# Weight products of the second attention by head, the work in both passages between stages put in another order, and the router in one pass

## The reference

```python
x = x + attn(layernorm(x))            # 16 heads of 128, windowed, difference of two softmaxes
x = x + xattn(layernorm(x), ctx)      # 16 heads, low-rank keys and values from ctx
x = x + ffn(layernorm(x))             # 16 experts of 176, top 6, and a shared expert of 352

# xattn, per head h
q_big = rope((hidden @ Wq_h.T) @ w_kc_q_h)        # 256 -> 128 -> 192
q_r, k_r = q_big @ W_qr_h, rope(ctx) @ W_kr_h     # 192 -> 64, 64 -> 64
attn = softmax(q_r @ k_r.T)
out += (attn @ rope(ctx)) @ w_kc_kv_h.T @ Wo_h.T

# ffn
probs = softmax(xf @ gate_w.T)                    # 16 experts
combine = probs where among the top 6 of a token, else 0
moe = sum_e combine[:, e] * (silu(g_e) * u_e) @ w2_e.T
```

## Time and profile before

| | |
|---|---|
| Median of 3 runs | 1394.78 us (1394.64 to 1397.84) |
| The profiled execution | 1395.27 us, span 1393.4 us |
| TensorE busy | 1309.9 us, 94% of the span |
| VectorE, ScalarE, POOL busy | 847.0, 722.3, 470.7 us |
| Mean granted TensorE clock | 0.978 of full speed |
| Bytes by DMA | 64.57 MB, mean 46 GB/s |
| The chain that ended last | PE 71%, issue 12%, DVE 6%, ACT 4%, POOL 4%, DMA 2%, SPq 1% |

### The profile page before, as it was taken

The page is one execution under the profiler, slowest core; times in us unless marked ns, Lnnn a source line. Parts: engine busy times, 40 slices in busy tenths (PEclk is TensorE's granted clock), DMA queues, the critical chain, the costliest instruction groups (busy, mean ns, idle before and its releaser), DMA issues.

```text
span 1393.4 us, 27992 instructions
## 1 busy us (share of the span) xinstructions
PE 1309.9 (94%) x9948; PEld 1026.1 (74%) x9948; DVE 847.0 (61%) x1985; ACT 722.3 (52%) x2767; POOL 470.7 (34%) x466
## 2 busy tenths in 40 slices
PE   5899999999999888999999999959999999999998
PEld 3677887887887765666676666548888888888887
DVE  7788788787887576646646656755443343333433
ACT  2788887887887554444444444453333242333322
POOL 3222122212211134534534534550044253432532
PEclk9899999999999899999999999988999999999999
DMA  6011002000102101001002001010134234253130
GB/s 213 16 32 39 17 17 54 17 16 16 32 16 88 34 1 73 1 2 73 2 1 72 1 1 59 1 40 18 33 70 132 63 93 90 38 132 75 43 100 30
DMA packets 29684, 64.57 MB, mean 46 GB/s; under 512 B 6784, under 2 KB 12032, under 8 KB 28288
## 3 DMA queue, kind: packets, MB, share of 16 engines
q1 hardware_dynamic: 29568, 63.05, 16.3%
HBM read 52.42 MB, written 2.23 MB: 39 GB/s over the span
## 4 chain that ended last, share of the span: by engine, by line
PE 71%; issue 12%; DVE 6%; ACT 4%; POOL 4%; DMA 2%; SPq 1%; POOLq 0%; DVEq 0%; ACTq 0%
PE ps L515 30%; PE ps L879 9%; PE ps L698 4%; PE ps L802 4%; PE ps L631 4%; PE ps L663 3%; PE ps L792 3%; PE ps L776 3%; PE ps L784 2%; PE ps L674 2%; POOL ea L1622 2%; PE ps L654 2%; DMA cw<-comb_d 2%; ACT ea L1392 1%; PE ps L570 1%
## 5 line engine op out<-in xcount | busy, mean ns | idle before, releaser
L1751 POOL TENSOR_TENSOR sg<-sg,cw 128x512 f32<-128x512 f32 x88 | 113.6, 1291 | 278.6 <-ACT sg L1558 270.6
L1333 DVE TENSOR_TENSOR hh<-ps,sg 128x512 f32<-128x512 f32 x100 | 69.2, 692 | 182.1 <-POOL sg L1751 165.6
L1359 ACT ACTIVATE hhh<-hh 128x512 fp32r<-128x512 f32 x100 | 63.2, 632 | 209.0 <-DVE hh L1333 198.2
L1359 ACT ACTIVATE pt<-ps 128x512 f32<-128x512 f32 x128 | 76.8, 600 | 179.3 <-PE ps L784 112.9
L1392 ACT ACTIVATE ea<-ps,negmax 128x64 f32<-128x64 f32 (+1 forms) x512 | 164.6, 341 | 6.0 <-DVE negmax L1085 6.0
L515 PE MATMUL ps<-xnh,wch 128*128 128x512 f32 x400 | 159.6, 399 | 0.5 <-DVE x_sb L1046 0.5
L515 PE MATMUL ps<-xnh,wcl 128*128 128x512 f32 x400 | 159.3, 398 | 0.0
L515 PE MATMUL ps<-xnl,wch 128*128 128x512 f32 x400 | 158.5, 396 | 0.0
L1132 DVE TENSOR_TENSOR qcs<-ps,tabb 128x512 f32<-128x512 f32 x192 | 123.5, 686 | 54.6 <-PE ps L515 54.2
L1622 POOL TENSOR_TENSOR ea<-ea,rden 128x128 f32<-128x128 f32 (+1 forms) x128 | 62.2, 507 | 230.8 <-DVE rden L1041 230.8
L1629 POOL TENSOR_TENSOR eb<-eb,rsum 128x512 f32<-128x512 f32 x64 | 66.5, 1039 | 172.7 <-DVE rsum L1172 172.7
(11 more groups left out here) (149 smaller groups left out, 3436.6 us busy)
## 6 DMA issues: line engine op xcount, KB each, us to landing
raw_w<-in_rawb_dram SPq DMA_DIRECT2D x4, 2432.0 KB, 9.4
kva<-ktmp SPq DMA_DIRECT2D x64, 128.0 KB, 2.3
cw<-comb_d SPq DMA_DIRECT2D x32, 256.0 KB, 4.8
raw_w<-in_rawc_dram SPq DMA_DIRECT2D x4, 1920.0 KB, 8.1
cw<-comb_d SPq DMA_DIRECT2D x16, 224.0 KB, 4.2
raw_a<-in_wqk_dram SPq DMA_DIRECT2D x4, 768.0 KB, 4.5
cw<-comb_d SPq DMA_DIRECT2D x16, 192.0 KB, 5.9
cw<-comb_d SPq DMA_DIRECT2D x16, 160.0 KB, 5.5
```

Of the source, the lines that this page charges most:

```text
L1333: dve.tensor_tensor(hh[:, par, :], bank(C_U[par]), sg[:, par, :], ALU.mult).then_inc(c_h, 1)
L1359: return act.activation(dst, src, ACT.Copy)
L1751: pool.tensor_tensor(sg[:, par, :], sg[:, par, :], cw[:, c % 2, t, :], ALU.mult).then_inc(c_hs, 1)
```

## The change

`b_prep` makes wb by head: items 0 to 3 are the heads, two products of 192 columns each into columns 0 to 383 of a bank; ScalarE and VectorE scatter them into the row tiles in two copies and two subtractions (`b_split`, `b_columns`). Items 4 and 5 make mq for three tiles each, and VectorE alone copies it. The slots of the items in the loop stay.

The passage from A to B: chunk 4's turns go to unit 12, the six items to slots 0 and 1 of units 13 to 15, three of four context transposes to unit 15, slot 2, with banks 0, 1 and 7; the rest, qb 0 to 3 and chunk 5's turns to the second drain unit. Chunk 6's turns go to B's units 0 and 1 and chunk 7's to units 4 and 5.

The passage from B to C: chunk 9's turns go to unit 14; the first gate and up products stand in the second drain unit, the gate product between the last transposes and PV; chunks 10 and 11 are turned at k = 1 and 3. ScalarE and POOL prepare three of the five weight tiles before C and two in its first pairs. The wait for B's additions moves behind the products of k = 1.

The router takes all 16 sequences at once: the padded gate weight (32 columns) is the stationary operand, the 512 tokens of a chunk move, and the four chunks go to four column strips of one bank, at k = 4; four transposes bring the logits back to token order at k = 5; one chain of 16 steps on 256 columns; all four combine transposes at k = 8, ahead of the down product there. SP loads the next weights after the first spread instead of before the first store.

```diff
-                   ("final", 11, 0): [("ln", 4, 0)], ("final", 11, 1): [("ln", 4, 1)],
-                   ("final", 12, 0): [("prep", 0)], ("final", 12, 1): [("prep", 1)],
-                   ("final", 13, 0): [("prep", 2)], ("final", 13, 1): [("prep", 3)], ("final", 13, 2): [("prep", 4)],
-                   ("final", 14, 0): [("prep", 5)], ("final", 14, 1): [("ln", 5, 0)], ("final", 14, 2): [("ln", 5, 1)],
-                   ("final", 15, 1): [("kt2", 0)], ("final", 15, 2): [("kt2", 1)],
-                   ("drain", 0, 1): [("qb", 0), ("qb", 1), ("kt2", 2)], ("drain", 0, 2): [("kt2", 3)],
-                   ("drain", 1, 0): [("ln", 6, 0)], ("drain", 1, 1): [("qb", 2), ("qb", 3)],
-                   ("drain", 1, 2): [("ln", 6, 1)]}
+                   ("final", 12, 0): [("ln", 4, 0)], ("final", 12, 1): [("ln", 4, 1)],
+                   ("final", 13, 0): [("prep", 0)], ("final", 13, 1): [("prep", 1)],
+                   ("final", 14, 0): [("prep", 2)], ("final", 14, 1): [("prep", 3)],
+                   ("final", 15, 0): [("prep", 4)], ("final", 15, 1): [("prep", 5)],
+                   ("final", 15, 2): [("kt2", 0), ("kt2", 1), ("kt2", 2)],
+                   ("drain", 1, 0): [("kt2", 3), ("qb", 0)], ("drain", 1, 1): [("qb", 1)],
+                   ("drain", 1, 2): [("qb", 2), ("qb", 3), ("ln", 5, 0), ("ln", 5, 1)]}
...
-                   ("final", 12, 1): [("ln", 9, 0, 7), ("ln", 9, 1, 2)],
-                   ("drain", 0, 2): [("ln", 10, 0, 2), ("ln", 10, 1, 3)]}
+                   ("final", 14, 2): [("ln", 9, 0, 7), ("ln", 9, 1, 3)]}
...
             def b_prep(g_to, t, bk):
...
+                if t < HG:
+                    for kt in range(KT):
+                        last = pe.matmul(bk[:, XQ * kt:XQ * (kt + 1)],
+                                         raw_b[:, RB_WQ + t * DM + 128 * kt:RB_WQ + t * DM + 128 * (kt + 1)],
+                                         raw_b[:, RB_KCQ + t * XQ:RB_KCQ + (t + 1) * XQ], start=True, stop=True)
+                    return last
+                for k in range(XT // 2):
+                    for h, a, w, row in b_segments(XT // 2 * (t - HG) + k):
...
+                if drain and u == 1:
+                    c_up(0, 0, 0, 0)
...
+            def c_logits():
 
                 pe.wait_ge(c_gws, 16)
+                pe.wait_ge(ln_h, 3 * NC * KT)
+                for kt in range(KT):
+                    for c in range(NC):
+                        last = pe.matmul(ps[EQ * c:EQ * (c + 1), C_X[0], :], gw[:, kt, :], xnf[:, kt, CW * c:CW * (c + 1)],
+                                         start=kt == 0, stop=kt == KT - 1, skip_group_check=True)
...
+            def c_turn():
+
+                pe.wait_ge(c_gs, GATE_STEPS)
...
+                if first and k == 1:
+                    pe.wait_ge(b_y, NG * UN)
+                if first and k in (1, 3):
...
+                if first and k == 4:
+                    c_logits()
+                if first and k == 5:
+                    c_token_major()
+                if first and k == 8:
+                    c_turn()
...
-            ln_stats(2 * NC - 1)
-            dve.wait_ge(a_wo, NG * UN)
+            dve.wait_ge(a_tp, NG * UN)
             item = XT + 4
             for what in B_FIRST[item:]:
+                if what[0] == "qr":
+                    ln_low(5)
+                    ln_stats(6)
+                    dve.wait_ge(a_wo, NG * UN)
...
+                if first and k == 0:
+                    ln_norm(3 * NC - 1)
+                if first and k in (2, 4):
+                    ln_low(2 * NC + 1 + k // 2)
+                if first and k == 5:
+                    gate_take()
+                if first and 5 <= k < 8:
+                    gate(k - 5)
...
+            ln_low(2 * NC + 1)
+            c_low(0, 1)
+            c_low(0, 2)
+            ln_rstd(3 * NC - 1)
+            ln_low(2 * NC + 2)
+            ln_low(3 * NC - 1)
+            for t in range(SH_N, TG):
                 c_low(0, t)
```

More of the change, by code:

```diff
@@ L49 @@
 GATE_STEPS = 16
-GP = 2
-GB = B // GP
+EQ = 32
 RC_T = 2 * KT * 128 + DM
@@ L543, in pj_taken @@
                     pe.wait_ge(b_if, what[1] + 1)
-                else:
-                    pe.wait_ge(b_kvc, what[1] + 1)
             def b_turn(r):
                 pe.wait_ge(b_kv, 5)
+                if r < 2:
+                    pe.wait_ge(a_ex, NG * UN - 1)
+                elif r == 2:
+                    pj_taken(held.pop())
+                else:
+                    pe.wait_ge(b_kvc, 1)
                 for j in range(CB):
-                    last = pe.transpose(quads(bank(PJ))[:, j, :], kvr[:, CB * r + j, :, :], idf[:, :])
+                    last = pe.transpose(quads(bank(kt_bank(r)))[:, j, :], kvr[:, CB * r + j, :, :], idf[:, :])
                 last.then_inc(b_kvp, 1)
@@ L797, in b_unit @@
                         pe.wait_ge(b_if, b_item(g, 2, 2, ("wco", 1)) + 1)
+                    if first and u == 3:
+                        pe.wait_ge(a_y, NG * UN)
                     pe.wait_ge(b_ol, n - 2)
@@ L804, in b_unit @@
                     last.then_inc(b_wo, 1)
+                if drain and u == 1:
+                    c_up(0, 0, 0, 0)
                 slot(2)
-            def c_logits(p, bk):
-                pe.wait_ge(c_gws, 16)
-                pe.wait_ge(ln_f, (2 * NC + (p + 1) * NC // GP) * KT)
-                for i in range(GB):
-                    b = GB * p + i
-                    for kt in range(KT):
-                        last = pe.matmul(ps[:, bk, E * i:E * (i + 1)], xnf[:, kt, S * b:S * (b + 1)], gw[:, kt, :],
-                                         start=kt == 0, stop=kt == KT - 1)
-                last.then_inc(c_lg, 1)
@@ new lines, in c_token_major @@
+            def c_token_major():
+                pe.wait_ge(c_lt, 1)
+                for j in range(CB):
+                    last = pe.transpose(quads(bank(C_X[1]))[:, j, :], glt[:, S * j:S * (j + 1)], idf[:, :])
+                last.then_inc(c_lm, 1)
+            def c_turn():
+                pe.wait_ge(c_gs, GATE_STEPS)
+                for r in range(NC):
+                    last = pe.matmul(ps[0:CB * E, C_X[0], S * r:S * (r + 1)], gp[:, CB * r:CB * (r + 1), :], idf[:, :],
+                                     start=True, stop=True)
+                last.then_inc(c_ct, 1)
@@ L1173, in b_unit @@
                 slot(1)
+                if final and u == 15:
+                    ln_stats(10)
+                if drain and u == 0:
+                    ln_low(9)
+                if drain and u == 1:
+                    ln_norm(10)
                 if not (first and u < 3):
@@ L1176, in b_unit @@
                 slot(2)
+                if first and u in (2, 6):
+                    ln_low(2 * NC - 2 + u // 4)
                 if first and u == 2:
-                    ln_low(2 * NC - 1)
+                    ln_stats(2 * NC - 1)
+                if first and u == 3:
+                    ln_norm(2 * NC - 1)
                 if final and u == 7:
@@ L1235, in gate @@
                 elif i == 1:
-                    dve.wait_ge(c_ge, p + 1)
-                    step(dve.tensor_reduce(gsum[:, bs], ge[:, bs, :], axis=AX.X, op=ALU.add))
-                    step(dve.reciprocal(grec[:, bs], gsum[:, bs]))
-                    step(dve.tensor_tensor(gp[:, bs, :], ge[:, bs, :], over_e(grec[:, bs]), ALU.mult))
-                    for b in range(GB * p, GB * (p + 1)):
+                    dve.wait_ge(c_ge, 1)
+                    step(dve.tensor_reduce(gsum[:, :], ge[:, :, :], axis=AX.X, op=ALU.add))
@@ L1462, in b_take @@
                         bk = bank(2 + par)
-                    copy(wbh[:, t, :, :].rearrange("p k n -> p (k n)"), bk[:, 0:256])
-                    copy(mq[:, t, :], bk[:, 256:384]).then_inc(b_m, 1)
+                    for high, src in zip(b_split(wbh, t), b_columns(bk)):
+                        last = copy(high, src)
+                    last.then_inc(b_m, 1)
                 elif kind == "wco":
@@ L1500, in b_unit @@
                 slot(2)
-                if first and u < KT:
-                    ln_take(2 * NC - 1, u, QRB)
+                if first and u in (0, 1, 4, 5):
+                    ln_take(2 * NC - 2 + u // 4, u % 4, QRB)
             def c_high(g_to, t):
@@ L1558, in c_unit @@
                 act.activation(sg[:, par, :], bank(C_G[par]), ACT.Silu).then_inc(c_sg, 1)
-                if first and k in (7, 11):
-                    for i in range(2):
-                        c_take_comb((k - 7) // 2 + i, C_X[i])
                 act.wait_ge(c_h, v + 1)
```

287 lines of the change are left out of this document (140 added, 147 removed).

## The result

The changed kernel takes 1363.3 us (median of 4 runs, 1355.4 to 1363.8) beside 1395.7 for the kernel before: ratio 0.9749, 95% interval 0.9725 to 0.9774. In a second series on another occasion it took 1363.3 beside 1395.9, 0.9764 (0.9751 to 0.9777). So it is 32 to 33 us faster, where 42.2 were forecast. Its profiled execution took 1363.3 (span 1361.5, granted clock 0.983; before 0.978). TensorE is busy for 1279.0 us instead of 1309.9, still 94% of the span.

The account below looks back on a forecast made before the run. TensorE's work was taken to bound the loop, and its waits for other engines and lowered clock the two passages. Gains of 12.8 + 13.4 + 16.0 = 42.2 us led to 1352.6 us as a median, range 1341 to 1366.

Parts of the forecast that it names:

- rival (b): Both attentions' last units or first feed-forward tiles: ScalarE's order bites harder, 12 us less gain, 1364.6 us; chance 0.15.
- Loop, 12.8: Second attention's loop: three rebuilds of the weight products each gain 4.3 us, 12.8 us together (10 to 15).
- The stall in unit 11: Loop, unit 11: three items back to back on two banks make TensorE wait, charged 0.7 us a turn.
- First passage, 13.4: Passage from stage A to B: second attention's first scores 17.4 us earlier net, less 4 for clock: 13.4 us (8 to 18).
- The clock, charged with 4.0: First passage: clock falls after three remaining waits of 2 to 3 us would cost 4 us.
- the walk: First passage stepped through on the old clock: second attention's first scores at 513.1 instead of 531.5.
- The five waits: First passage, TensorE: 2.1, 3.2 and 2.6 us before units' products, 1.5 before the out product, 2.0 before the contraction.
- Second passage and router, 16.0: Passage to the feed-forward and its first tiles, router included: 16 us gained (11 to 21) after clock charges.
- the new wait: Router: TensorE waits 4.5 us (2 to 6) for VectorE's last gate step ahead of the combine transposes.
- (a): Both passages: the clock does not fall, as work stands closer; the clock charges come back, 1345.5 us; chance 0.17.
- (c): Router and products: strips run one after another (+5), 192-column records cost 0.21 (+3.2); 1361 us; chance 0.08.
- (d): Feed-forward's first pass: TensorE stays at 1.2 GHz after the 4.5 us wait; slower, 1437 us; chance 0.02.

Follow-up runs that it names:

- e4: Kernel before with only the weight products made by head, in the old slots: 1381.1 us, ratio 0.9897 to the kernel before.
- e1: Changed kernel with VectorE's first context rotation waiting only for its own two loads, not all sixteen: 1357.5 us, ratio 0.9726 to the kernel before.
- e2: Changed kernel with the combine transposes one pair later, at k = 9 instead of 8: 1355.8 us, ratio 0.9718 to the kernel before.
- yardstick: The changed kernel run once more, unaltered, beside follow-up kernels on the same chip: 1363.3 us, ratio 0.9764 to the kernel before.
- e6: Changed kernel with the old first passage, keeping products by head, second passage and router: 1360.0 us, ratio 0.9741 to the kernel before.
- e12: Changed kernel with both the own wait of the first context rotation and the combine transposes at k = 9: 1351.4 us, ratio 0.9686 to the kernel before.
- e8: On top of e12, VectorE's statistics of chunk 7 moved behind the residual of the second attention's unit 3: 1349.9 us, ratio 0.9671 to the kernel before.
- e9: e6 (old first passage) with the combine transposes at k = 9: 1356.1 us, ratio 0.9716 to the kernel before.
- e3: Kernel before with the gate weight's tile allocated 32 columns wide, later tiles 128 bytes per partition higher: 1393.0 us, ratio 0.9974 to the kernel before.
- e7: On top of e12, turns and products of stage A's last units reordered so ScalarE-copied items stand in other slots: 1356.6 us, ratio 0.9704 to the kernel before.
- e10: On top of e8, POOL's residuals of weight tiles 3 and 4 put ahead of its chunk 11 residual: 1348.1 us, ratio 0.9658 to the kernel before.

## Why the prediction was right or wrong

The time, 1363.3, lies in the range of 1341 to 1366, near the sum of rival (b), 1364.6, and 10.7 above the forecast. The loop and the second passage came as forecast, of the first passage's 13.4 us 2.6 did. Point by point:

**Loop, 12.8: right.** From the first product of a rebuild to unit 13's scores it took 16.6 us before (597.20 to 613.79) and 12.5 after (595.81 to 608.33): 4.1 a turn, 4.3 forecast. Two of its terms were off and cancelled, which is luck. From start to start the sixteen records of the heads take 3.5 us (1.79, 0.97 and 0.74), 0.22 each, where 0.16 was taken and 0.21 was the upper bound; the mq records cost 0.70 + 0.95 instead of 2.3. The stall in unit 11 is 0.49 (0.7 charged). e4 shows the three turns together, 12.7.

**First passage, 13.4: wrong, measured 6.9 (91.5 to 84.6), and 2.6 with its price of 4.3 in stage B.** Three steps failed.
- VectorE's wait for the tables. Unit 12 was walked with "ScalarE's unit of 5 to 6 us setting the pace", and its scores came at 453.6 behind stage A's 1.5, as forecast (453.7). But VectorE wasn't walked. Its first context rotation stood in unit 12 before as well; there unit 12 came later, and the statistics of chunk 5 ran ahead of it. The change brought it forward to 458.4, while SP still issues the fourteen table loads one after another until 462.7. The prediction looked at these loads' queue only for the moved gw load at its end. Price: 3.4 us of waits of TensorE in the passage, 5.8 us in all with the clock (e1).
- The clock, charged with 4.0, and the work itself. Without the charge the walk takes 73.1 us from unit 10's scores, 13.0 of it named waits, which leaves some 60.1 of work. After, TensorE works for 68.9 and is without work for 15.7. In e2, with the same code there and hardly a fall of the clock (0.98), it worked for 63.3. So the falls stretched the work by some 5.6 us more than in e2, and some 3 us of work at full clock were missing from the walk; which ones the runs don't separate. By time the falls cost less, 4.2 (84.9 to 80.7), since the waits grew (16.1 in the yardstick, 17.4 in e2). The five waits named were right to within 0.4 us, and with VectorE's wait gone the idle time is the walk's (12.7 in e1, 13.0). A sign of the clock is the last contraction, 3.64 us behind a wait of 2.28, and 1.95 in e2 behind the same wait.
- Chunk 6's and 7's move into the second attention's first units was priced at 1.0, the transposes alone. It cost 4.3 (75.1 us from the first scores to unit 12's in the yardstick, 70.8 in e6). In e1 and e12, with the same code there but no fall of the clock, it takes 73.1, so 2.0 are the half clock behind a wait for VectorE's residual (a contraction of 3.14 for 1.95). e8 takes 71.3: 1.8 are VectorE's statistics ahead of that residual, the wait itself. The transposes are the remaining 0.6, less than their 1.0. The prediction counted what the moved step costs TensorE and not what it puts into VectorE's queue.

What the order itself gives, when these are mended, is the difference of e8 and e9: 1349.9 against 1356.1, 6.2 us; the forecast had 9.4.

**Second passage and router, 16.0: right.** 471.2 became 454.7, and stage B's last four units gave 1.2 (13.4 to 12.2 us): 17.6. The 1.2 is not clearly the new order's, as e4 took 12.4 with the old one. Of the 17.6 up to 2.6 is the pad of e3, which the prediction didn't have, so some 15.0 by its own steps. That the pad helped is luck. e6 and e4 give a second reading, as they differ only in the second passage, the router and the pad: 15.7 behind unit 10's scores (15.5 in the rest, 0.8 in stage B, less 0.6 in the first passage), so 13 to 14 without the pad. No run takes the second passage and the router apart. The feed-forward starts 7.8 us after unit 15's scores (under 9 forecast), the normalisation beside POOL took 4.44 (4 taken, bounds 1.4 and 5.6), the down product of tile 0 waits 1.03 (0.5), the logits take 1.92 (1.9: the four strips run side by side), a gate step of 256 columns 0.46 (0.46), MAX8 1.32 (1.4), the new wait 4.06 (4.5, bounds 2 and 6). The clock didn't fall in the last units, only behind the new wait, where 2.1 were charged: transposes and down product took 4.6 (962.64 to 967.26), where 2.5 is what they take at full clock (1.09 in e2, and twelve records at 0.12).
By the rule of the Trainium skill (SBUF — State Buffer, "SBUF: two separate sides") the normalisation would last as long as POOL's operations beside it. POOL's two weight residuals ran from 914.17 to 917.85 and the normalisation from 914.21 to 918.65, 0.8 beyond them, and the same operation took 1.38 at 924.77 with POOL idle: the trace agrees. The 1.6 us more that the rule gave in the prediction were for three operations beside it; the third was over by then.

**Rivals.** (a) no fall of the clock: true for the last units of stage B, false for the first passage, except for e2's execution. (b) had the right size for a partly right reason: waits behind ScalarE did bite, but at the sizes of the forecast, and e7 shows one other order of them that gains little; the missing time came from VectorE's queue, the clock and work that the walk had too short. (c) fell for the strips, which run side by side; its records of 0.21 came true, but the mq records made up for them. (d) fell: the half clock behind the 4.06 us wait ended within 6 us. Its argument "a fall after waits is certain" doesn't hold either: in e2 TensorE waited 3.24 and 3.06 us in the first passage and the granted clock stayed at 1.00 from 465 to 515.

**Not in the prediction at all:** stage A, whose code is unchanged, took 1.5 us more.

## What to carry to other kernels

A step that gets earlier must be walked on every engine, and against the loads that it waits for: a wait on one semaphore for sixteen transfers, harmless for a unit that comes late, held up an engine with everything queued behind it, and a semaphore of its own for the two that matter gave 5.8 us, the clock's part included. A moved normalisation is priced by its statistics on VectorE and its place before a residual, not by its transposes. And before a result of a few microseconds is put down to an edit, cut the span at an event ahead of it: here the unchanged first 440 us differed by up to 5.3 us between kernels, and the same code of the first passage by 4.2 between two executions.

## What the runs showed of the hardware that was not expected

- **Where tiles lie changes the rate of the products.** 128 bytes more per partition ahead of all later tiles: 0.2331 to 0.2292 us for a product of 512 columns in the feed-forward, 2.6 us of the whole time. In stage B's loop it does much less: a turn from unit 12's scores to the next group's takes 102.72 us before and 102.53 with the pad. So it isn't every operand alike; which tile's place matters was not tried.
- **The clock falls at different places for the same code.** In stage A the granted clock is below 1 around 35, 45 to 55, 330 and 435 us in the kernel before and e6, and in e2 at the first three of these; around 45 to 55, 105 to 115, 220 and 435 in after, e1, e12 and e8. Executions of one kernel differ too: e2 1350.3 to 1359.1 at granted clocks of 0.992 to 0.984, e7 in two clusters 5.8 us apart. e2 and after have the same code up to the first combine transposes and differ from 35 us on. Nor does a wait settle it: a wait of 2.06 us had a fall around it in after (scores of 2.67 us behind it), one of 3.24 in e2 had none. What picks the pattern stays open; no run separates it.
- **VectorE's operations on SBUF alone stand while POOL works, those with a PSUM input don't.** `hhl` 2.37 and `xnl` 2.33 beside POOL instead of 0.69, and the long ones move with POOL's instruction (e10). The attention residual of e10 at 903.25 (`x_sb`, 0.42) and `obl` at 903.59 (0.41), which read PSUM, have their usual length beside POOL's residual of 902.65 to 903.93. The Trainium skill (SBUF — State Buffer, "SBUF: two separate sides") states this for operations with two SBUF inputs; the trace agrees, and e10 shows it by moving the cause.
